# The small steps of the mLSTM head norm move from VectorE to GpSimd, all but the absolute value and the maximum

## What is computed

```python
normalizer = jnp.maximum(jnp.abs(jnp.sum(C, axis=-1, keepdims=True)), jnp.exp(-max_log_D))
h = jnp.einsum('bhst,bhtd->bhsd', C / (normalizer + EPS), vh)      # EPS = 1e-6
mean = jnp.mean(h, axis=-1, keepdims=True)
var = jnp.mean((h - mean) ** 2, axis=-1, keepdims=True)
h_norm = (h - mean) * jax.lax.rsqrt(var + 1e-05)
...
x = _layernorm(x + attention(x))
x = _layernorm(x + mlstm(x, ctx))
x = _layernorm(x + ffn(x))
```

## Time and profile before

| | |
|---|---|
| median of three runs | 715.84 us (715.34 to 716.31) |
| the profiled execution, its own time | 711.05 us |
| span of its instructions | 709.3 us |
| mean granted TensorE clock | 0.961 of full speed |
| busy: TensorE, VectorE, ScalarE, GpSimd | 87%, 87%, 80%, 71% of the span |

### The profile page before, as it was taken

How to read it: one execution, slowest core, us unless ns; L and a number is a source line. 1 busy time by engine, 2 the same in 40 slices (tenths; PEclk the granted TensorE clock), 3 DMA queues, 4 the chain that set the end, 5 groups by cost and what they waited for, 6 DMA issues and landing times. The chain is left out here.

```text
span 709.3 us, 16642 instructions
## 1 busy us (share of the span) xinstructions
PE 614.1 (87%) x4892; PEld 451.7 (64%) x4892; DVE 618.5 (87%) x2387; ACT 566.2 (80%) x1189; POOL 506.6 (71%) x781
## 2 busy tenths in 40 slices
PE   5578999999999999999999998999999979784642
PEld 4365676777768686867677675868676757552311
DVE  4466788999999999999999999999999999885853
ACT  3157978999898989888889988998989878966431
POOL 4176696969877887878888888888778865744322
PEclk9989999999999999999999999999999999997865
DMA  6999873465646462736556663846353641221101
GB/s 200 155 227 180 110 135 61 82 113 121 106 88 107 102 118 59 134 55 110 85 93 73 143 98 65 145 76 111 75 120 56 117 79 41 51 61 46 44 16 44
DMA packets 106104, 69.20 MB, mean 98 GB/s; under 512 B 47200, under 2 KB 106016, under 8 KB 106016
## 3 DMA queue, kind: packets, MB, share of 16 engines
q1 hardware_dynamic: 106016, 68.14, 53.0%
HBM read 28.73 MB, written 4.26 MB: 47 GB/s over the span
## 5 line engine op out<-in xcount | busy, mean ns | idle before, releaser
L1854 DVE CUSTOM_DVE_ANT_0 sc<-pS,bias 128x256 f32<-128x256 f32 x512 | 194.7, 416 | 26.9 <-PE pS L291 22.3
L1040 POOL TENSOR_SCALAR sc<-sc,mx 128x256 f32<-128x256 f32 x336 | 167.6, 511 | 12.1 <-DVE mx L1854 11.6
L1317 ACT ACTIVATE pr<-pT 128x512 f32<-128x512 f32 x256 | 147.5, 602 | 11.9 <-PE pT L309 10.9
L309 PE MATMUL pT<-ident,sc 128*128 128x128 f32 x1024 | 148.6, 275 | 7.0 <-ACT pr L1317 3.7
L309 PEld LDWEIGHTS pT<-ident,sc 128*128 128x128 f32 x1024 | 119.1, 142 | 26.2 <-issue 10.4
L291 PE MATMUL pS<-ks,qs 96*128 96x256 bf16 x512 | 93.1, 278 | 22.5 <-DVE mx L1854 16.6
L1305 ACT ACTIVATE sc<-sc,mx 128x256 f32<-128x256 f32 x176 | 84.1, 514 | 6.9 <-DVE mx L1854 6.9
L291 PEld LDWEIGHTS pS<-ks,qs 96*128 96x128 bf16 x512 | 44.5, 99 | 53.6 <-DVE mx L1854 31.9
L326 PE MATMUL pO<-pr,va 128*32 128x256 f32 x1024 | 68.5, 385 | 0.5 <-ACT oT L1327 0.5
L1007 POOL TENSOR_TENSOR rs<-ve,minus_half 128x2 f32<-128x2 f32 x48 | 34.3, 715 | 44.0 <-DVE ve L1885 43.7
L1062 POOL TENSOR_SCALAR hq<-h 128x512 bf16<-128x512 f32 x64 | 38.6, 621 | 30.7 <-ACT h L1516 28.7
(11 more groups left out here) (291 smaller groups left out, 1680.8 us busy)
## 6 DMA issues: line engine op xcount, KB each, us to landing
qs<-parts SPq DMA_DIRECT2D x96, 128.0 KB, 4.6
ks<-parts SPq DMA_DIRECT2D x96, 128.0 KB, 5.2
mb<-mrows SPq DMA_DIRECT2D x16, 512.0 KB, 3.9
xin<-in_x SPq DMA_DIRECT2D x16, 256.0 KB, 4.6
xb<-in_x SPq DMA_DIRECT2D x16, 256.0 KB, 3.4
cx<-in_ctx SPq DMA_DIRECT2D x32, 128.0 KB, 2.1
out<-hq SPq DMA_DIRECT2D x16, 256.0 KB, 2.3
bias<-in_L_attn_pos_bias SPq DMA_DIRECT2D x4, 768.0 KB, 8.0
```

The lines of the kernel that those rows point to most:

```text
L309: ins = pe.transpose(bank[:, kt * S + t * P:kt * S + t * P + P], sc[:, s % RING, t, kt * P:kt * P + P], ident[:])
L1040: ins = pool.tensor_scalar(sc[:, s % RING, t, :], sc[:, s % RING, t, :], -1.0, mx[:, s % RING, t:t + 1], ALU.mult, ALU.add)
L1317: act.activation(flat(pr[:, s % RING, :, :]), pT[s % 2][:, :], ACT.Exp, scale=-1.0)\
L1854: dve.tensor_tensor_reduce(out=sc[:, s % RING, t, :], in0=pS[s % 2][:, t * S:t * S + S], in1=bias[:, s, t * P:t * P + S][:, ::-1], scale=1 ...
```

## The change

Seven of the eight steps that move are the same arithmetic on GpSimd (`head_moments` there): both sums and the difference, the floor, the two squares, the variance. What VectorE does as a scalar-tensor-tensor with a constant is split: a factor is folded into the neighbouring steps (`head_floor` scales by 2 x sqrt(1e-5), the variance becomes four times its value, and `head_norm` multiplies by 2 as a scalar-tensor-tensor), and one step is new, the sums of squares times 4/64. So 8 VectorE instructions of a batch go and 9 GpSimd instructions come, 128 and 144 in the program. VectorE keeps the absolute value and the maximum, which now stand in a row in `head_bound`.

`head_centred` on VectorE waits for the third of the nine steps, GpSimd's fourth step waits for VectorE's maximum, and `head_rstd` waits for the ninth.

```diff
-            def head_moments(f):
-                dve.wait_ge(gn_v.sem, gn_v.at(f, 8))
-                dve.tensor_tensor(hmv[:, 0, :, :], half(1, 0), half(1, 1), ALU.add).then_inc(gn_v.sem, 1)
-                dve.tensor_tensor(hmv[:, 1, :, :], half(1, 0), half(1, 1), ALU.subtract).then_inc(gn_v.sem, 1)
-                dve.tensor_tensor(hmv[:, 2, :, :], half(2, 0), half(2, 1), ALU.add).then_inc(gn_v.sem, 1)
...
+            def head_moments(f):
+                pool.wait_ge(gn_v.sem, gn_v.at(f, 8))
+                pool.tensor_tensor(hmv[:, 1, :, :], half(1, 0), half(1, 1), ALU.subtract).then_inc(hm_g.sem, 1)
+                pool.tensor_tensor(hmv[:, 2, :, :], half(2, 0), half(2, 1), ALU.add).then_inc(hm_g.sem, 1)
+                wait(pool, yc_v, f - 1, 1)
+                pool.tensor_tensor(hmv[:, 0, :, :], half(1, 0), half(1, 1), ALU.add).then_inc(hm_g.sem, 1)
+                pool.wait_ge(nm_v.sem, nm_v.at(f, 2))
+                pool.tensor_scalar(nrm[:, 2, :, :], nrm[:, 1, :, :], 1e-6, 2.0 * 1e-5 ** 0.5, ALU.add, ALU.mult)\
+                    .then_inc(hm_g.sem, 1)
+                pool.wait_ge(hm_g.sem, hm_g.at(f, 1))
+                pool.tensor_tensor(hmv[:, 3, :, :], hmv[:, 1, :, :], hmv[:, 1, :, :], ALU.mult).then_inc(hm_g.sem, 1)
+                pool.wait_ge(hm_g.sem, hm_g.at(f, 2))
+                pool.tensor_scalar(hmv[:, 5, :, :], hmv[:, 2, :, :], 4.0 / XD, None, ALU.mult).then_inc(hm_g.sem, 1)
+                pool.wait_ge(hm_g.sem, hm_g.at(f, 4))
+                pool.tensor_tensor(nrm[:, 3, :, :], nrm[:, 2, :, :], nrm[:, 2, :, :], ALU.mult).then_inc(hm_g.sem, 1)
+                pool.wait_ge(hm_g.sem, hm_g.at(f, 6))
+                pool.tensor_tensor(hmv[:, 4, :, :], hmv[:, 3, :, :], hmv[:, 5, :, :], ALU.add).then_inc(hm_g.sem, 1)
+                pool.wait_ge(hm_g.sem, hm_g.at(f, 8))
+                pool.tensor_tensor(nrm[:, 5, :, :], hmv[:, 4, :, :], nrm[:, 3, :, :], ALU.add).then_inc(hm_g.sem, 1)
...
             def head_rstd(f):
-                pool.wait_ge(gn_v.sem, gn_v.at(f, 15))
+                pool.wait_ge(hm_g.sem, hm_g.at(f, 9))
+                wait(pool, hn_v, f - 1, 1)
...
             def head_bound(f, par):
                 dve.wait_ge(am_a.sem, am_a.at(f, 2))
-                dve.wait_ge(gn_v.sem, gn_v.at(f, 12))
+                dve.wait_ge(cv_sb.sem, cv_sb.at(f, XH))
+                wait(dve, hm_g, f - 1, 4)
+                dve.scalar_tensor_tensor(nrm[:, 0, :, :], total, -1.0, total, ALU.mult, ALU.max).then_inc(nm_v.sem, 1)
+                dve.wait_ge(nm_v.sem, nm_v.at(f, 1))
                 dve.tensor_tensor(nrm[:, 1, :, :], nrm[:, 0, :, :], emT[:, par, :, :], ALU.max).then_inc(nm_v.sem, 1)
-            def head_floor(f):
-            def head_scale(f):
-            def head_scaled(f):
...
             def head_centred(f):
-                dve.wait_ge(gn_v.sem, gn_v.at(f, 14))
+                dve.wait_ge(hm_g.sem, hm_g.at(f, 3))
...
             def head_norm(f):
-                dve.tensor_tensor(y, y, per_head(nrm[:, 7, :, :]), ALU.mult).then_inc(gn_v.sem, 1)
+                dve.scalar_tensor_tensor(y, y, 2.0, per_head(nrm[:, 7, :, :]), ALU.mult, ALU.mult).then_inc(hn_v.sem, 1)
...
-                inner_quantised(1, 1); negated(4, 8); rstd(3, 0); negated(4, 9); head_rstd(2); mem_scaled(2)
+                inner_quantised(1, 1); negated(4, 8); rstd(3, 0); negated(4, 9); head_moments(2); head_rstd(2)
```

More of the change, by code:

```diff
@@ L1075, in output @@
                 ins.then_inc(out_g.sem, 1)
+            def head_moments(f):
+                if not live(f):
+                    return
+                half = lambda k, part: hst[:, :, :, 3 * part + k]
+                pool.wait_ge(gn_v.sem, gn_v.at(f, 8))
[16 more added lines that the diff above has]
+                pool.tensor_tensor(nrm[:, 5, :, :], hmv[:, 4, :, :], nrm[:, 3, :, :], ALU.add).then_inc(hm_g.sem, 1)
             def head_rstd(f):
@@ L1453, in mem_out @@
                     wait(act, yc_v, c - 1, 1)
+                    wait(act, nm_v, c - 1, 2)
                 act.activation(cv[:, :, hh, :], bank_of(f"cv{hh}", c)[:, 0:S].rearrange("p (t d) -> p t d", t=TT)
@@ new lines, in from_batch_15 @@
+                row_shift(14, 0); head_centred(13); biased(15, 8, 1); biased(15, 9, 0); ffn_residual(12, 0)
+                head_norm(13); biased(15, 9, 1); biased(15, 10, 0); biased(15, 10, 1); biased(15, 11, 0)
+                biased(15, 11, 1); biased(15, 12, 0); biased(15, 12, 1); row_stats(13, 1); biased(15, 13, 0)
+                row_moments(13, 1); row_eps(13, 1); ffn_residual(12, 1); biased(15, 13, 1); row_shift(13, 1)
+                forget_sums(14); row_max(13); running_max(14); row_max_bounded(13); row_inverse(13); row_scale(13)
@@ L2477, in from_batch_15 @@
-                row_moments(15, 2); row_eps(15, 2); row_shift(15, 2)
+                attention_residual(15); head_bound(14, 0); row_stats(15, 0); row_moments(15, 0); row_eps(15, 0)
+                row_shift(15, 0); ffn_residual(13, 0); head_centred(14); head_norm(14); row_stats(14, 1)
+                row_moments(14, 1); row_eps(14, 1); row_shift(14, 1); ffn_residual(13, 1); forget_sums(15)
+                row_max(14); row_max_bounded(14); row_inverse(14); row_scale(14); running_max(15); row_factors(14)
@@ new lines, in from_batch_15 @@
+                head_stats(15, 2); head_stats(15, 3); head_bound(15, 1); head_centred(15); head_norm(15)
+                row_stats(15, 1); row_moments(15, 1); row_eps(15, 1); ffn_residual(14, 0); ffn_residual(14, 1)
+                row_shift(15, 1); row_stats(14, 2); row_moments(14, 2); row_max(15); row_max_bounded(15)
+                row_inverse(15); row_eps(14, 2); row_scale(15); row_factors(15); row_shift(14, 2); gated(15, 0)
+                gated_up(15, 0); gated(15, 1); gated_up(15, 1); inner_max(15, 0); gated(15, 2); inner_bound(15, 0)
```

326 lines of the change are left out of this document (134 added, 192 removed).

## The result

The changed kernel takes 742.83 us (median of four runs, 741.95 to 745.52), the kernel before 715.59 beside it (714.76 to 716.31): 1.039 times as long, with a 95% interval of 1.036 to 1.042. That is some 27 us more, within the range and on the side forecast, but nearly twice the 15.7 us of the sum. The profiled execution took 743.58 us, its span is 741.8.

What follows compares the result with a forecast made beforehand. VectorE was taken as the bound. `head_norm` starting 1.39 us later a batch, 20.9 us in fifteen, less 5.2 given back, made +15.7 us, carried over to 731.6 us; the range was 715 to 745.

Steps and rivals of the forecast that it cites:

- the sum: Over fifteen batches: 20.9 us from later `head_norm` starts less 5.2 given back, +15.7 us on the profiled execution.
- The bound: VectorE, busy 36.57 of 37.60 us a batch; time taken from it helps only if it then has something to do.
- The price of a step: Nine GpSimd steps of 128 x 8: 0.29 us with two inputs, 0.185 with one, together 2.4 us.
- Waits between the steps: Within the GpSimd block: two links wait for the step just ahead, 0.08 us each, made good by overlapping starts.
- Conflicts: GpSimd steps held up beside VectorE's `head_centred`: 0.2 us a batch, with 0 and 0.4 as ends.
- The block: The nine GpSimd steps ahead of the power, conflicts included: 2.6 us a batch.
- The shift: Later start of `head_norm`: +1.54, +1.20 and +1.44 us in batches 8, 1 and 6, mean 1.39 a batch.
- The earlier `ve`: Removed VectorE steps bring `ve` 1.17 us earlier; GpSimd uses 0.70, 0.51 and 1.17 in batches 8, 1 and 6.
- the give-back: Behind `head_norm`, small waits for TensorE that a later VectorE no longer meets: 0.35 us a batch, 5.2 in fifteen.
- a TensorE that starves: Rival: late `negated` steps behind the block make TensorE's transposes wait, adding 12 us, to 744 us; chance 0.10.
- Cheap steps: Rival: small GpSimd steps cost 0.13 us or less, memset 0.114, and the kernel gets faster, 712.7 us; chance 0.16.
- What would show it: Profile signs: GpSimd busy some 38 us more, VectorE some 25 less, about 45 idle before `head_norm`, `rs` waits nearly unchanged.

Runs made afterwards that it cites:

- experiment 2: The changed kernel without the nine GpSimd steps, nothing in place of VectorE's eight, variance and mean left out of the output: 710.92 us, 0.9944 of the kernel before.
- experiment 3: The changed kernel with `head_centred` waiting for the ninth GpSimd step instead of the third: 748.28 us, 1.0465 times the kernel before.
- experiment 1: The kernel before with the nine GpSimd steps added on scratch ahead of the power, VectorE keeping its eight: 751.63 us, 1.0506 times the kernel before.

## Why the forecast was right, and what was mis-sized

- **The bound.** Right, with a limit. VectorE ends up waiting, and the batch grows by its waits. The prediction asked whether VectorE would have something to do; experiment 2 answers it: 17.2 us off VectorE are 4.0 off the kernel. The Trainium skill ("Perfetto Trace Analysis", "Identifying the Most-Contended Engine") says to optimise the engine with the highest occupancy first. Here that engine was busy for 36.57 of 37.60 us, and experiment 2 shows how little of it could be cashed.
- **The price of a step.** 0.20 to 0.24 us, two inputs or one, in place of 0.29 and 0.185. Nine of them on their own would be under 1.9 us, not 2.4. The dearer fit was wrong since its fixed 0.276 us, taken from long steps, doesn't hold for eight elements.
- **Waits between the steps.** 0.08 us each, as read, but at five or six of the nine, not two, and the overlap makes them good only among the first three.
- **Conflicts.** 0.5 us in every batch in place of 0.2 in the mean: the step that starts while `head_centred` runs is held until it ends (428.00 for 0.71 us in batch 8, and the 2.18 us of experiment 3). In the kernel before only three of sixteen powers met it. By the Trainium skill's rule ("Advanced Engine Details and Errata", "GPSIMD Details") a VectorE instruction with two SBUF inputs conflicts with GpSimd; the runs agree, in every batch, and the price is nearer the 0.4 worked out from that rule than my 0.2.
- **The block.** 2.7 us for 2.6: three wrong terms that cancelled, which is luck. The Trainium skill's factor of two for two-input work ("GPSIMD Engine Reference", "Engine selection") is not what a step of eight elements shows: 0.20 us against VectorE's 0.16 is 1.25.
- **The shift.** Right. Without an earlier `ve` the prediction's three batches give 2.24, 1.71 and 2.61, a mean of 2.19 us; the traces have 2.12 (5.41 less 3.28, unrounded), with the slack of 0.4 us found and used. The block alone is then 33 us by the prediction's working, and 36 in experiment 1.
- **The earlier `ve` and the give-back: here it failed.** The sum counted 0.79 us a batch (0.70, 0.51 and 1.17 used) for `ve` and 0.35 for waits that VectorE would no longer meet, 17 us in fifteen batches. From `head_norm` to `ve` the batch became 0.09 us shorter, and experiment 1 parts the two terms. The give-back: its block alone, with nothing removed, makes this stretch 0.29 us longer (34.89 after 34.60), so nothing is given back. Right behind `head_norm` VectorE does lose the other waits that it had before, 0.33 us a batch, of which 0.03 are left in experiment 1. But the second layer norm's statistics cannot start sooner than GpSimd's two passes over `y` behind `head_norm` (1.27 and 1.28 us in batch 8, at 431.98 and 433.33), and there VectorE waits instead: 0.55 us a batch in experiment 1 and 0.57 in the kernel after, 0.07 before. The earlier `ve`: the removal makes the stretch 0.38 us shorter (34.89 to 34.51), where the sum had 0.79. The five removed steps had filled time in which VectorE would have waited: with them gone the attention's residual sum waits 0.32 us a batch for TensorE, 0.03 before and in experiment 1. All in all the removal was worth 9 us against experiment 1, 4 by itself.
- **The range.** It holds the result by 2 us, and its upper end had been set for a TensorE that starves, which didn't come. That the time lies within is owed in part to a margin meant for something else.
- **The rivals.** Cheap steps were half true: 0.20 is cheap, but not 0.13, and the steps' waits and the hold-up make up for it. TensorE is not starved by late `negated` steps: its weight loads wait 2.8 us for them in 4 times from 104 to 620 us, about as before (3.4 in 2).
- **What would show it.** GpSimd's busy time rose by 33 us (38 forecast), VectorE's fell by 18 (25), `rs` still waits 39.6 us for `ve` (43.7 before), and `head_norm` waits 32.4 us (45). All signs were right, and the forecasts of the first, second and last too large by 15 to 40%.

The maximum on VectorE (L1946, right behind the absolute value now) takes 386 ns in the mean where it took 287, 1.6 us in all. In the kernel after it starts beside an `hq` or a `negated` of GpSimd in ten of sixteen batches and ends 0.01 to 0.02 us behind that step's end; before, it did so in eight, mostly from a later start.

## What to carry to other kernels

An engine that is busy for 97% of a stretch is not a bound that every removed step relaxes: look at what each step's successor would wait for if it came sooner, since small steps can stand in waits that the trace doesn't show as waits, as five did here. A block that is moved to an engine with 18% of idle time is not free there: none of the places tried took it for nothing. What goes beyond the wait that it lies in is added to the next hand-over, and the price is read from who waits for that. Where two engines hand work to and fro, a small step is cheap on the one that would wait without it, as VectorE would have here.

## Of the hardware, not expected

- A GpSimd step on 128 x 8 elements takes 0.20 to 0.24 us, independent ones start 0.17 us apart, and one that has to wait for a semaphore starts about 0.08 us behind the end of the step ahead. The power on the same eight values takes 1.65.
- The hold-up beside VectorE's two-input `head_centred` goes by who starts second. A GpSimd step that starts within it ends behind it (0.20 becomes 0.71, 1.65 becomes 2.18). The other way round it depends on GpSimd's step. In the kernel before 39 of VectorE's 160 steps on 128 x 8 took over 0.25 us, and 38 of these ended 0.01 to 0.03 us behind the end of a GpSimd step beside them, an `hq` or a `negated` for the most part (line 1947 in the earlier trace rows ends at 411.39, beside the first of the two `hq` of the earlier trace rows, which together take 1.21 us from 410.76). Beside a power nothing is held: in the kernel before `head_centred` started 0.15 to 1.12 us into the power in eleven of sixteen batches, and took 0.68 or 0.69 us as ever, the power 1.65, and of VectorE's small steps those that started beside the layer norm's power took 0.15 to 0.19 us. In three batches `head_centred` started 0.16 to 0.23 us ahead of the power, and the power took 2.02 to 2.08. The Trainium skill ("SBUF — State Buffer", "SBUF: two separate sides") says that whichever of the two starts first has the shared ports for its whole instruction and the other is blocked. Both halves agree with these runs, but for a power that starts first. Why it doesn't hold VectorE stays open.
